# Graph diffusion on one core: f16 parts for the logits and the first step's products, and a new order of turning, products and logits

## What is computed

```
q = X @ W1.T @ W2.T;  k = X @ W3.T               # 64 features each
for n in range(2):
    probs = softmax(q @ k.T, axis=-1)            # from the current Xa, 2708 x 2708
    A  = probs kept down to the top 0.9 of each row's sum, rows rescaled to 1
    Xf = R @ Xf                                  # R: adjacency plus identity, rows rescaled
    Xa = A @ Xa
    Z  = Z + Xf @ U1[n].T + Xa @ U2[n].T
h = X + Z                                        # then layer norm
```

## Time and profile before

| | us |
|---|---|
| median of 3 runs | 3489.43 (3483.46 to 3489.57) |
| the profiled execution | 3485.84 |
| its span, first to last instruction | 3484.1 |

### The profile page before, as it was taken

The page is one execution under the profiler, slowest core; times in us unless marked ns, Lnnn a source line. Parts: engine busy times, 40 slices in busy tenths (PEclk is TensorE's granted clock), DMA queues, the critical chain, the costliest instruction groups (busy, mean ns, idle before and its releaser), DMA issues. The chain is left out here.

```text
span 3484.1 us, 47349 instructions
## 1 busy us (share of the span) xinstructions
PE 2571.7 (74%) x14938; PEld 1846.5 (53%) x14938; DVE 2124.2 (61%) x5181; ACT 1283.8 (37%) x2109; POOL 574.6 (16%) x1501
## 2 busy tenths in 40 slices
PE   3388878849575999896874556587855339999999
PEld 2366666638453777675651445465644314444458
DVE  5566766641325666667134777876787567777751
ACT  4345445320325656463126545465641140000000
POOL 0000000000003333231004534444640000000000
PEclk9699989979775999898975778788977759999999
DMA  1212112002100000000100000000000120000013
GB/s 39 102 63 83 62 62 82 30 24 62 44 14 1 22 16 20 16 19 16 49 15 0 9 9 10 9 9 13 13 9 9 36 97 1 0 0 0 0 31 94
DMA packets 44330, 104.10 MB, mean 30 GB/s; under 512 B 5584, under 2 KB 24304, under 8 KB 41328
## 3 DMA queue, kind: packets, MB, share of 16 engines
q1 hardware_dynamic: 44144, 102.05, 9.2%
HBM read 85.46 MB, written 16.58 MB: 29 GB/s over the span
## 5 line engine op out<-in xcount | busy, mean ns | idle before, releaser
L1182 PE MATMUL bank<-kT,step_queries 64*128 64x512 f32 x528 | 284.2, 691 | 317.0 <-ACT step_E L1249 301.5
L1681 DVE SCALAR_TENSOR_TENSOR fil_acc<-bank,fil_node,fil_acc 128x256 f32<-128x256 f32 x682 | 330.1, 484 | 110.2 <-PE bank L1754 97.4
L1182 PEld LDWEIGHTS bank<-kT,step_queries 64*128 64x128 f32 x528 | 107.1, 227 | 492.2 <-ACT step_E L1249 414.6
L1249 ACT ACTIVATE step_E<-bank 128x512 f32<-128x512 f32 (+1 forms) x264 | 137.4, 545 | 410.9 <-PE bank L1182 208.6
L1752 PE MATMUL bank<-fil_wh,fil_xTh 128*128 128x512 f16 x704 | 268.3, 381 | 0.0
L1753 PE MATMUL bank<-fil_wl,fil_xTh 128*128 128x512 f16 x704 | 268.0, 381 | 0.0
L1754 PE MATMUL bank<-fil_wh,fil_xTl 128*128 128x512 f16 x704 | 267.8, 380 | 0.0
L1269 ACT ACTIVATE step_junk<-step_E,step_first 128x2708 fp8e4<-128x2708 f32 x88 | 224.6, 2552 | 15.1 <-ACT step_bell L1276 9.6
L1199 PE MATMUL bank<-A,step_PT 128*128 128x256 f32 x968 | 212.6, 379 | 0.8 <-ACT step_PT L1240 0.8
L1199 PE MATMUL bank<-H,step_PT 128*128 128x256 f32 x968 | 212.6, 379 | 0.5 <-ACT step_PT L1240 0.5
L1362 DVE MAX8 step_top<-step_E 128x8 f32<-128x2708 f32 x44 | 131.2, 2982 | 132.3 <-ACT step_E L1249 127.8
(11 more groups left out here) (337 smaller groups left out, 5483.9 us busy)
## 6 DMA issues: line engine op xcount, KB each, us to landing
gat_A<-in_adj SPq DMA_DIRECT2D x22, 1408.0 KB, 6.5
step_a<-adjT SPq DMA_DIRECT2D x44, 352.0 KB, 3.1
fil_raw<-in_L_W SPq DMA_DIRECT2D x16, 512.0 KB, 4.6
adjT<-gat_a SPq DMA_DIRECT2D x22, 352.0 KB, 6.8
gcn_a<-adjT SPq DMA_DIRECT2D x22, 352.0 KB, 2.9
out_a<-adjT SPq DMA_DIRECT2D x22, 352.0 KB, 3.0
X<-in_x SPq DMA_DIRECT2D x1, 2816.0 KB, 11.2
x_kept<-X SPq DMA_DIRECT2D x1, 2816.0 KB, 9.9
```

Of the source, the lines that this page charges most:

```text
L1182: pe.matmul(l_bank[n % 2][:, 0:m], queries[q][half, :], kT[half, c:c + m], start=True, stop=True).then_inc(l_ready, 1)
L1249: act.activation(E[q][j][:, c:c + m], l_bank[n % 2][:, 0:m], ACT.Copy).then_inc(l_done, 1)
L1681: c(dve.scalar_tensor_tensor(out=acc[k][:], in0=ps, scalar=node[k][:, n:n + 1], in1=acc[k][:], op0=ALU.mult, op1=ALU.add))
```

## The change

Keys and queries are kept as f16 parts (high and low, of 64 times the value). `kH` and `kL` hold each key's part on both halves of the partitions; `qHL` has the query's high part on partitions 0 to 63 and the low part on 64 to 127. Two f16 matmuls over 128 partitions give the logits. In `keys` ScalarE writes the two high parts and VectorE the two low ones, and a copy of the query in f32. The copies of the query by GpSimd in the steps go.

In step0 the kept probabilities are turned into two f16 parts: `turned` writes the high one, the new `lows` on VectorE the low one, and the bank is free when `lows` has read it. `attend` takes three f16 matmuls a block, with the features' f16 parts that are there already. `finish` of step0 adds into H; the stores to `pending`, its load and the 22 additions in keys1 go.

In both steps the order on TensorE and ScalarE is new: `turn` (`products` on ScalarE) first, then the transposes (`turned`), then `mix` and the logits.

```diff
-def keys(core, name, src, kT, qT, shape, W1, W2, W3, x_kept=None, pending=None):
+def keys(core, name, src, kH, kL, qHL, shape, W1, W2, W3, x_kept=None, plain=False):
...
-                reuse(pe, k_done, t, 2)
+                reuse(pe, k_done, t, 3)
...
+            def high(t, k):
+                act.wait_ge(q_ready, t + 1)
+                act.activation(cols(kH, t, 128), k_bank[k][:, 0:128], ACT.Copy, scale=SQ).then_inc(q_hi, 1)
+                act.activation(cols(qHL, t, 128), k_bank[k][:, 128:256], ACT.Copy, scale=SQ).then_inc(q_hi, 1)
+
+            pipelined(act, [(0, evacuate), (1, rows), (2, high)])
...
-                dve.wait_ge(q_ready, t + 1)
-                dve.tensor_scalar(kT[:, bass.ds(t * 128, 128)], k_bank[k][:, 0:128], 1.0, None,
-                                  ALU.mult).then_inc(k_done, 1)
...
+                    dve.wait_ge(q_hi, t * 2 + 2)
+                    dve.scalar_tensor_tensor(out=cols(kL, t, 128), in0=ps[:, 0:128], scalar=SQ, in1=cols(kH, t, 128),
+                                             op0=ALU.mult, op1=ALU.subtract).then_inc(k_done, 1)
+                    q_lo = qHL[DA:, bass.ds(t * 128, 128)]
+                    dve.scalar_tensor_tensor(out=q_lo, in0=ps[DA:, 128:256], scalar=SQ, in1=q_lo,
+                                             op0=ALU.mult, op1=ALU.subtract).then_inc(k_done, 1)
...
-            if plain:
-                dve.wait_ge(fetched, 16)
-                for t in range(T):
-                    dve.tensor_tensor(cols(core.H, t), cols(core.H, t), cols(core.X, t), ALU.add)
...
+        low_done = sem("low_done")
+        bank_read = low_done if parts else pT_done
...
-                    pe.wait_ge(pT_done, t * NCH + n + 1 - nb)
+                    pe.wait_ge(bank_read, t * NCH + n + 1 - nb)
...
-                half = slice(j * DA, j * DA + DA)
-                if n == 0 and j == 0:
-                    pe.wait_ge(q_ready, p + 1)
-                pe.matmul(l_bank[n % 2][:, 0:m], queries[q][half, :], kT[half, c:c + m],
-                          start=True, stop=True).then_inc(l_ready, 1)
+                for part, k in enumerate((kH, kL)):
+                    last = pe.matmul(l_bank[n % 2][:, 0:m], cols(qHL, t, 128), k[:, c:c + m],
+                                     start=part == 0, stop=part == 1)
+                last.then_inc(l_ready, 1)
...
+                pe.wait_ge(bank_read, t * NCH + NCH)
+                if parts:
+                    last = probabilities_times(pe, pvf_bank[j][:, 0:D], PhT, PlT, srcA)
...
-            pipelined(pe, [(2, lambda p, q: neighbours(p, 0)), *chunks(0), (3, lambda p, q: turn(p, 1)),
-                           (3, lambda p, q: mix(p, 1)), (2, lambda p, q: attend(p, 0)),
-                           (2, lambda p, q: neighbours(p, 1)), *chunks(1), (2, lambda p, q: turn(p, 0)),
-                           (2, lambda p, q: mix(p, 0)), (2, lambda p, q: attend(p, 1))], T // 2)
+            pipelined(pe, [(2, lambda p, q: neighbours(p, 0)), (3, lambda p, q: turn(p, 1)),
+                           (2, lambda p, q: all_transposes(p, 0)), (3, lambda p, q: mix(p, 1)),
+                           (0, lambda p, q: all_logits(p, q, 0)), (2, lambda p, q: attend(p, 0)),
+                           (2, lambda p, q: neighbours(p, 1)), (2, lambda p, q: turn(p, 0)),
+                           (2, lambda p, q: all_transposes(p, 1)), (2, lambda p, q: mix(p, 0)),
+                           (0, lambda p, q: all_logits(p, q, 1)), (2, lambda p, q: attend(p, 1))], T // 2)
...
             if evals == 1:
-                pipelined(act, [*chunks(0), (3, lambda p, q: products(p, 1)),
-                                (0, lambda p, q: exponentials(p, q, 0)), (0, lambda p, q: first_sums(p, q, 0)),
-                                *chunks(1), (2, lambda p, q: products(p, 0)),
-                                (0, lambda p, q: exponentials(p, q, 1)), (0, lambda p, q: first_sums(p, q, 1))],
-                          T // 2)
+                pipelined(act, [products_1, turned_0, logits_0, exponentials_0, first_0,
+                                products_0, turned_1, logits_1, exponentials_1, first_1], T // 2)
             else:
...
+                pipelined(act, [products_1, turned_0, logits_0, exponentials_0, second_1, first_0,
+                                products_0, turned_1, logits_1, exponentials_1, second_0, first_1], T // 2)
...
+            def lows(p, j):
+                t = p * 2 + j
+                for n, (b, m) in enumerate(CHUNKS):
+                    dve.wait_ge(pT_done, t * NCH + n + 1)
+                    dve.scalar_tensor_tensor(out=PlT[:, b * 128:(b + m) * 128],
+                                             in0=p_bank[n % len(p_bank)][:, 0:m * 128], scalar=SP,
+                                             in1=PhT[:, b * 128:(b + m) * 128],
+                                             op0=ALU.mult, op1=ALU.subtract).then_inc(low_done, 1)
...
-                pipelined(dve, [take_1, below_0, largest_0, below_1, finish_1,
-                                take_0, sort, keep_0, largest_1, keep_1, finish_0, check], T // 2)
+                pipelined(dve, [take_1, lows_0, below_0, largest_0, below_1, finish_1,
+                                take_0, lows_1, sort, keep_0, largest_1, keep_1, finish_0, check], T // 2)
```

More of the change, by code:

```diff
@@ L42 @@
 SW = 4096.0
+SQ = 64.0
 EPS = 1e-5
@@ L791, in keys @@
     centre, spread, top, rise = shape
-    plain = pending is not None
     paced = unrolled if plain else pipelined
@@ L882, in _ @@
             pe.wait_ge(gram_done, 2)
-            pe.wait_ge(k_done, 2 * T)
+            pe.wait_ge(k_done, 3 * T)
             core.fence(pe)
@@ L978, in diffusion_step @@
     centre, spread, top, rise = shape
+    parts = srcA is srcF
     with nc.cleanup_on_exit(), ExitStack() as ctx:
@@ L999, in diffusion_step @@
         PT = sb("PT", [128, NP])
-        z = [sb(f"z{k}", [128, D]) for k in range(2 if pending is not None else 0)]
+        PhT, PlT = (PT[:].bitcast(F16)[:, i * NP:i * NP + NP] for i in range(2))
         a8 = [sb(f"a8{k}", [128, NP], F8) for k in range(2)]
@@ L1043, in load @@
                                  adjT8[bass.ds(t * 128, 128), :]).then_inc(a8_loaded[j], 16)
[L1045 to L1055 removed]
+            pipelined(sp, [(1, load)], T // 2)
         @block.gpsimd
@@ L1093, in guess @@
                 pool.wait_ge(guessed, t * 2 + 2)
-            def query(p, q):
-                if not (isinstance(p, int) and p < 2):
-                    pool.wait_ge(l_ready, (p * 2 - 2) * NL)
-                pool.tensor_copy(queries[q][:], cols(qT, p, 128)).then_inc(q_ready, 1)
             def excess(c, q, j, S):
@@ L1196, in attend @@
                 t = p * 2 + j
-                pe.wait_ge(pT_done, t * NCH + NCH)
-                for i in range(T):
-                    last = pe.matmul(pvf_bank[j][:, 0:D], PT[:, i * 128:i * 128 + 128], srcA[:, i * D:i * D + D],
-                                     start=i == 0, stop=i == T - 1)
+                pe.wait_ge(bank_read, t * NCH + NCH)
+                if parts:
+                    last = probabilities_times(pe, pvf_bank[j][:, 0:D], PhT, PlT, srcA)
+                else:
+                    for i in range(T):
+                        last = pe.matmul(pvf_bank[j][:, 0:D], PT[:, i * 128:i * 128 + 128],
+                                         srcA[:, i * D:i * D + D], start=i == 0, stop=i == T - 1)
                 last.then_inc(pv_ready, 1)
@@ new lines, in all_evacuated @@
+                    evacuate(p, q, j, n)
+            products_0, products_1 = (2, lambda p, q: products(p, 0)), (3, lambda p, q: products(p, 1))
+            turned_0, turned_1 = ((2, lambda p, q, j=j: rows_turned(p, j)) for j in range(2))
+            logits_0, logits_1 = ((0, lambda p, q, j=j: all_evacuated(p, q, j)) for j in range(2))
+            exponentials_0, exponentials_1 = ((0, lambda p, q, j=j: exponentials(p, q, j)) for j in range(2))
+            first_0, first_1 = ((0, lambda p, q, j=j: first_sums(p, q, j)) for j in range(2))
```

111 lines of the change are left out of this document (45 added, 66 removed).

## The result

The changed kernel takes 3610.94 us in the median of four executions (3600.88 to 3622.57), the one before 3487.90 beside it. The ratio is 1.036, 95% interval 1.034 to 1.037. That is 123 us more where the prediction had 73, and it lies above the range (3503 to 3600). The profiled execution took 3613.49 us, 127.7 more than the profiled one of before (3485.84).

The account below looks back on a forecast made before the run. Step 0 was taken as bound by TensorE, step 1 by GpSimd's threshold wait and an equally long VectorE path. 29 + 12 + 5 + 26.5 = +73 on the profiled 3485.8, forecast 3560 us; 3503 to 3600 holds 8 in 10.

Parts of the forecast that it names:

- Keys, +12 and +5: Keys stages: added copies and operations cost 0.6 us a tile, +12 each stage; keys1 also saves 7 on dropped additions.
- The link: Keys: chain from query matmul over ScalarE and VectorE to `product` of the tile after next, 0.6 to 0.7 us longer.
- Step 0, +29: First diffusion step: pairs +38, first six tiles -5, tail -1, removed stores of `z` -3.
- The ring: Step 0: each half one serial chain, `largest`, sums, `products`, `turned`, `lows`, next `largest`; halves 28.6 and 27.35 us.
- the slow branch for the clock: Step 0: transposes at 1.2 GHz in every half, `lows` ending 6.05 us behind the sums, a pair 57.45.
- the fast branch: Step 0: transposes at 2.4 GHz, `lows` ending 5.3 us behind the sums, a pair 55.95.
- The idle time of 5 us: Step 0, a sign: TensorE stands idle 5 us ahead of `turn`, with granted clock under 1.0.
- the head's terms: Step 0, first six tiles: logits -2.7 for three tiles, -4.4 for the first, ring +7 and -2; carried as -5.
- Rival 2: Clock brings TensorE back onto the path: step 0 pair 59, clean checks cost 5, about 3590 us; chance 0.12.
- Step 1, +26.5: Second diffusion step: first tiles -7 from logits, new order after checks +33.5, the other half keeping its 26.8 us.
- Ties: Rival 4: f16 parts change the number of tie repairs from nine, each 19 us; chance 0.03.
- my case: Whole kernel: the summed forecast of +73 us, with its own range 3525 to 3595; chance 0.64.

Follow-up runs that it names:

- k_keys_warm: The changed kernel with five filler f16 matmuls (128x512, read by nobody) per tile in both keys stages: 3566.88 us, ratio 1.023.
- k_keys_wait: The changed kernel with `product` in keys waiting for the bank of keys only ahead of its last pair of matmuls: 3560.41 us, ratio 1.022.
- m_best: The changed kernel with k_keys_wait's edit, the old TensorE and ScalarE order, late `lows`, and `finish` ahead of `below_1` and `keep_1`: 3481.49 us, ratio 0.997.
- m_old_step1: The changed kernel with the old order on TensorE and ScalarE put back in the second step only: 3567.24 us, ratio 1.023.
- k_old_order: The changed kernel with the old order on TensorE and ScalarE in both steps, all f16 parts kept: 3616.10 us, ratio 1.037.
- n_best_warm2: m_best with two filler f16 matmuls (128x512, read by nobody) added per tile in the keys: 3412.37 us, ratio 0.979.

## Why the prediction was wrong

The sign and most of the mechanisms were right; the size failed in one step, the keys. By its own steps:

- **Keys, +12 and +5 (measured +43.6 and +42.0). This is the step that failed.** The link is where I said: the product waits for VectorE's last operation. It was sized a little low, 0.6 us a tile where it is 0.8 to 0.9 (a period of 3.6 to 3.9 at 2.4 GHz, where 3.5 was said). But I costed the added wait at its own length and put TensorE's clock in the keys at nothing. In the eighth tile the granted clock falls to 1.2 GHz and stays there; the period is then 5.4. k_keys_warm (2.4 GHz, the link kept: 116 and 118), k_keys_wait (2.4 GHz, no link: 94 and 94), m_best (1.2 GHz, no link: 135 and 136) and after (the link, and 1.2 GHz from the eighth tile on in keys0, from the fifth in keys1: 137 and 142) tell the two apart. As they came in after, at 0.8 to 0.9 us over 20 tiles 16 to 18 us a stage are the link's, the other 25 the clock's. Why the clock falls is only argued. I had given the clock a place in the steps, none in the keys.

  The Trainium skill (TensorE: Matmul & The Clock Gate, section HAM oscillation), which the prediction quotes, tells of waits for DMA between bursts, which the keys don't have. The next section of that page (A second HAM failure mode) describes small idle times between groups of matmuls that change banks; that is what these rows have, 0.7 to 1.1 us a tile ahead of `product`. It has the clock go to and fro, though, and here it falls once and stays down. m_best is at 1.2 GHz without such idle times, so they can't be the only cause.
- **Step 0, +29 (measured +31.7, about +51 with as many repairs).** The ring is right: VectorE's `lows` waits for ScalarE (3.51 us shown), ScalarE goes from sums to products without a hole, and `largest` starts 27.7 apart in one half where 27.35 was said. A pair is 58.9 where I took 56.7, 8 x 2.2 = 18 us. In number the slow branch for the clock (57.45) was nearer, but it is not what happened: in the rows around 1302 to 1360 the transposes run fast (12 in 1.47 us), and `lows` ends 5.3 us behind the sums in the shorter half, as in the fast branch. The other half, 30.3 where 28.6 was said, has the rest. There `neighbours` waits for `finish`, which I had not seen, then runs slow behind the idle time (6.49 us for 4.97), and ScalarE's products wait 1.2 us for `turn` behind it. The idle time of 5 us that I had forecast ahead of `turn` stands ahead of `neighbours` instead. The three long halves add about 0.7 to the mean of a pair. About 4 us lie in the head and the tail; the head's terms as I wrote them add up to -7.5, not to the -5 that I carried on, and it measured -4.1. Rival 2, a pair of 59, came out in its number; its place (TensorE's `mix` and logits behind `below_0`) did not: `largest` still follows VectorE's own work by 0.17.
- **Step 1, +26.5 (measured +12.0, about +31 with as many repairs).** Both halves of the sum were too small and cancel in part: the order costs 47 (m_old_step1), not 33.5, since the half that should have kept its 26.8 takes 27.85, most often with `largest` waiting 1.2 to 1.4 us for the logits copy. Half by half against m_old_step1, the nine halves behind a check cost 32 together, where I had 33.5; the nine others cost 11, where I had nothing, and 4 lie behind the last `largest`. The f16 logits give 16 beside the repair, not 7. With as many repairs the step is 5 us off, and that it is no more is luck.
- **Ties, two fewer.** Named as a rival with its price, 19 a repair; it happened within my case and took 38 off. Without it the miss would have been larger.
- **Sum.** Keys 85.6, step0 31.7, step1 12.0, ahead of them -1.7: 127.7 before rounding, the difference of the profiled executions.

What the prediction did not ask, and the experiments answer: the f16 parts in step0 aren't dear in themselves; in the place where `lows` was put they are. With `lows` behind `below_0` and `keep_0` and the old order, step0 is 20 us below what before takes without its repair (656.9 against 677.5), and the new order, which helps step0 by 47 only while `lows` stands in front, becomes needless.

## What to carry to other kernels

When a new operation goes into an in-order queue, ask what stands ready behind it and put it behind that; the same edit was worth 119 us with one order of the neighbouring engines and nothing with another, so the orders of all engines are to be chosen together. When a wait is added to a dense stretch of matmuls, look at TensorE's granted clock before and after, not only at the wait: here the period of a tile went from 2.9 to 3.7 with the wait and to 5.4 with the clock. Where a total hardly moves, compare by stages; k_old_order's 5 us hid -49 and +47.

## What the runs showed of the hardware

Filling TensorE with work that nobody reads made kernels faster: five matmuls a tile by 44 us (after against k_keys_warm), two a tile by 69 (m_best against n_best_warm2). And busy records alone don't tell whether the clock rises. The same kernel m_best had two times, 3442 to 3444 and 3480 to 3488; in its profiled execution the clock is 0.50 from 927 to 1062, with TensorE busy without a gap from 935 to 1031. The profiled execution of k_keys_wait, with the same code for the keys, rose to 2.4 GHz at about 938. Up to there TensorE does the same in both, from the first transpose on, 0.1 us apart. One row of each (m_best, then k_keys_wait) shows the first difference, in how long the same four matmuls take:

```profile
937.88 1.17 PE L865 MATMUL bank<-keys_xT,keys_WK 128*128 128x128 f32 x4
```

```profile
937.78 0.73 PE L865 MATMUL bank<-keys_xT,keys_WK 128*128 128x128 f32 x4
```

The Trainium skill (TensorE: Matmul & The Clock Gate, section What's actually happening) has the clock follow how busy TensorE has recently been; if busy means what these records count, the rows do not fit that. What decided between the two at the start of the stage stays open: the runs show only that two f16 matmuls more in each tile brought all five executions to between 3409.13 and 3415.49 us.
